# Context projections in 512-token blocks that cross batch borders, and a key-bias matmul with 128 weight rows

## The reference, cut to what matters

```python
ctx_txt = context[:, :TEXT_LEN, :]          # TEXT_LEN = 77
ctx_img = context[:, TEXT_LEN:, :]          # 179 tokens
k = (ctx_txt @ Wk).reshape(B, TEXT_LEN, HEADS, DIM_HEAD)
v = (ctx_txt @ Wv).reshape(B, TEXT_LEN, HEADS, DIM_HEAD)
k_ip = (ctx_img @ Wk_ip).reshape(B, Li, HEADS, DIM_HEAD)
v_ip = (ctx_img @ Wv_ip).reshape(B, Li, HEADS, DIM_HEAD)
...
qp = _proj(q, W1, b1, W2, b2)
kp = _proj(k, W1, b1, W2, b2)
qk = jnp.einsum('bqd,bkd->bqk', qp, kp) * scale + mask
attn = jax.nn.softmax(qk, axis=-1)
return jnp.einsum('bqk,bkd->bqd', attn, v1)
```

## Time and profile before

| | |
|---|---|
| median of 3 runs | 3375.27 us (3375.1 to 3377.76) |
| the profiled execution | 3377.16 us, of which its span 3375.4 us |
| PE busy | 3161.2 us, 94% of the span |
| PEld, DVE, ACT, POOL busy | 80%, 58%, 49%, 23% |
| projections, first matmul on a block to last | 23.3 to 445 us |
| masked attention, first turned tile to last matmul | 2328 to 2471 us |

### The profile page before, as it was taken

The page is one execution under the profiler, slowest core; times in us unless marked ns, Lnnn a source line. Parts: engine busy times, 40 slices in busy tenths (PEclk is TensorE's granted clock), DMA queues, the critical chain, the costliest instruction groups (busy, mean ns, idle before and its releaser), DMA issues. The chain is left out here.

```text
span 3375.4 us, 51188 instructions
## 1 busy us (share of the span) xinstructions
PE 3161.2 (94%) x16792; PEld 2696.3 (80%) x16792; DVE 1962.9 (58%) x3422; ACT 1667.3 (49%) x3204; POOL 789.5 (23%) x881
## 2 busy tenths in 40 slices
PE   7999979999999969999996798997979999999998
PEld 6988969999999958887884576885857888888886
DVE  3245549999999955557888995554752222222211
ACT  3132249999999943336776785564721111111110
POOL 0000038888888830000000200003700000000000
PEclk9999989999999989999997898998989999999999
DMA  6487755555555545556666686444831110001000
GB/s 187 120 253 228 224 171 165 170 177 173 170 165 173 157 150 198 179 172 203 226 218 219 215 265 218 158 161 165 251 116 60 38 35 24 31 26 38 32 25 13
DMA packets 370165, 503.46 MB, mean 149 GB/s; under 512 B 58940, under 2 KB 237420, under 8 KB 366032
## 3 DMA queue, kind: packets, MB, share of 16 engines
q1 hardware_dynamic: 356458, 473.37, 44.6%
q0 software_dynamic: 4768, 18.88, 1.7%
q10 hardware_dynamic: 8720, 8.41, 0.7%
HBM read 292.86 MB, written 174.11 MB: 138 GB/s over the span
## 5 line engine op out<-in xcount | busy, mean ns | idle before, releaser
L2592 DVE SCALAR_TENSOR_TENSOR lf_hT<-lf_hb,lf_hT 128x512 fp32r<-128x512 f32 x128 | 88.5, 691 | 571.6 <-ACT lf_hT L2668 571.6
L2668 ACT ACTIVATE lf_hT<-lf_hb 128x512 fp32r<-128x512 f32 x128 | 76.5, 598 | 669.2 <-PE lf_py L192 639.6
L768 POOL TENSOR_TENSOR at_prob<-at_prob,at_rec 128x308 f32<-128x308 f32 (+1 forms) x256 | 261.3, 1042 | 87.6 <-DVE at_rec L808 87.3
L908 ACT ACTIVATE at_prob<-at_sc,at_nm 128x77 f32<-128x77 f32 (+1 forms) x1024 | 277.6, 385 | 7.3 <-DVE at_nm L795 4.9
L190 PE MATMUL lf_hb<-lf_xT,lf_w 128*128 128x512 f32 x512 | 204.7, 400 | 1.3 <-DVE lf_hT L2592 1.3
L192 PE MATMUL lf_hb<-lf_xT,lf_w 128*128 128x512 f32 x512 | 203.5, 398 | 0.0
L190 PE MATMUL lf_py<-lf_w,lf_hT 128*128 128x512 f32 x512 | 203.1, 397 | 0.0
L192 PE MATMUL lf_py<-lf_w,lf_hT 128*128 128x512 f32 x512 | 203.1, 397 | 0.0
L191 PE MATMUL lf_hb<-lf_xT,lf_w 128*128 128x512 f32 x512 | 203.0, 396 | 0.0
L191 PE MATMUL lf_py<-lf_w,lf_hT 128*128 128x512 f32 x512 | 202.6, 396 | 0.0
L801 DVE TENSOR_REDUCE at_sums<-at_prob 128x4 f32<-128x308 f32 (+1 forms) x256 | 166.1, 676 | 17.7 <-ACT at_prob L908 17.5
(11 more groups left out here) (334 smaller groups left out, 9229.3 us busy)
## 6 DMA issues: line engine op xcount, KB each, us to landing
at_kr<-k_rows SPq DMA_DIRECT2D x256, 128.0 KB, 2.9
at_qs<-at_qst SPq DMA_DIRECT2D x512, 64.0 KB, 2.0
raw_gate<-pg_stage SPq DMA_DIRECT2D x96, 256.0 KB, 2.0
pu_rg<-raw_gate SPq DMA_DIRECT2D x96, 256.0 KB, 3.2
raw_up<-pu_stage SPq DMA_DIRECT2D x96, 256.0 KB, 2.1
om_raw<-raw_up SPq DMA_DIRECT2D x48, 512.0 KB, 4.5
dn_raw<-raw_up SPq DMA_DIRECT2D x48, 512.0 KB, 3.8
xn_parts<-pr_xturned SPq DMA_DIRECT2D x32, 512.0 KB, 5.0
```

The lines of the kernel that those rows point to most:

```text
L768: ins = pool.tensor_tensor(prob[:, i, :, lo:hi], prob[:, i, :, lo:hi], rec[:, z, g, :].unsqueeze(2).broadcast_to([P, 2 * NTE, hi - lo]), A ...
L908: ins = act.activation(prob[:, i, m, lo:hi], sc[n % 2][:, m, lo:hi], ACT.Exp, bias=nm[:, n % 2, g, m:m + 1])
L2592: dve.scalar_tensor_tensor(hT[:, i, 1, :], hb[i][:], 0.0, hT[:, i, 0, :].bitcast(F32), ALU.max, ALU.subtract).then_inc(h_done, 1)
L2668: act.activation(hT[:, m % 2, 0, :], hb[m % 2][:], ACT.Relu).then_inc(h_hi, 1)
```

## The change

Blocks no longer end with a batch: the text tokens (1232) become blocks of 512, 512 and 208, the image tokens (2864) five blocks of 512 and one of 304. Twelve blocks become nine, 168 jobs become 138, and 36 tiles become 33. The pieces of a tile now have whatever length the batch borders give. A key job is stored by one transfer for the whole batches and one more for each cut batch at its ends. The ring `stage` has 4 slots instead of 6, `xturned` 2 instead of 3. The `x` turns start with the second text block instead of the first image block, and the `w` turns stand three to a block in the last four blocks.

In the masked attention the weights `ones` have 128 rows, `trow` has 128 rows of which POOL clears all and the transfer fills two; POOL clears it ahead of its other work.

```diff
-TB, IB = 4, 2
...
 def context_blocks():
+
     blocks = []
-    for g in range(B // TB):
-        blocks.append(Rows("text", g * TB, TB * TEXT, [((g * TB + i) * S, TEXT) for i in range(TB)]))
-    for g in range(B // IB):
-        blocks.append(Rows("img", g * IB, IB * IMG, [((g * IB + i) * S + TEXT, IMG) for i in range(IB)]))
+    for kind, off, length in (("text", 0, TEXT), ("img", TEXT, IMG)):
+        every = Rows(kind, B * length, [(b * S + off, length) for b in range(B)])
+        for lo in range(0, every.n, CT):
+            n = min(CT, every.n - lo)
+            blocks.append(Rows(kind, n, [(row, count) for _, row, count in every.pieces(lo, n)]))
     return blocks
...
-    NBANK, NST, NRAW, NX = 6, 6, 3, 3
+    NBANK, NST, NRAW, NX = 6, 4, 3, 2
...
+    x_job = [first_job[1 + i] for i in range(NCH)]
+    x_by_job = {job: i for i, job in enumerate(x_job)}
+    WPER, WAT = 3, (5, 7, 11)
+    w_job = [first_job[NBLK - KF // WPER + i // WPER] + WAT[i % WPER] for i in range(KF)]
...
-    turns += [(first_job[NTX + i] + 5 + 2 * t, "x", i, t) for i in range(NCH) for t in range(NT)]
-    WFIRST, WPER, WAT = NTX + 2, KF // (NCH - 2), (6, 12)
-    turns += [(first_job[WFIRST + i // WPER] + WAT[i % WPER], "w", i, 0) for i in range(KF)]
+    turns += [(x_job[i] + 6 + 2 * t, "x", i, t) for i in range(NCH) for t in range(NT)]
+    turns += [(w_job[i], "w", i, 0) for i in range(KF)]
...
-                return [(k_d[job[1] * P:(job[1] + 1) * P, cols].rearrange("p (b n) -> p b n", n=S)[:, :, off:off + each],
-                         slot[:, 0:block.n].rearrange("p (b n) -> p b n", n=each))]
...
+                return out_ + [(k_d[rows_, row:row + count], slot[:, at:at + count]) for at, row, count in parts if count < each]
...
-        trow = ph.sb("trow", [2, B, S], F32R)
-        ones = ph.sb("ones", [2, P], F32R)
+        trow = ph.sb("trow", [P, B, S], F32R)
+        ones = ph.sb("ones", [P, P], F32R)
...
-            sp.dma_start(trow[:].bitcast(F32), split_d.rearrange("b a s -> a b s")).then_inc(t_ready, 16)
+            sp.wait_ge(trow_cleared, 1)
+            sp.dma_start(trow[0:2].bitcast(F32), split_d.rearrange("b a s -> a b s")).then_inc(t_ready, 16)
...
+            pool.memset(trow[:].rearrange("p b s -> p (b s)").bitcast(F32), 0.0).then_inc(trow_cleared, 1)
             pool.memset(ones[:].bitcast(F32), 1.0).then_inc(ones_made, 1)
```

More of the change, by code:

```diff
@@ L195, with __init__ @@
 IMG = S - TEXT
-TB, IB = 4, 2
 class Rows:
-    def __init__(self, kind, first, n, runs):
-        self.kind, self.first, self.n, self.runs = kind, first, n, runs
+    def __init__(self, kind, n, runs):
+        self.kind, self.n, self.runs = kind, n, runs
         self.tiles = [(lo, min(P, n - lo), max(0, lo + P - n)) for lo in range(0, n, P)]
@@ L246, in project_context @@
     blocks = context_blocks()
-    NBLK, NTX = len(blocks), B // TB
+    NBLK, NTX = len(blocks), sum(block.kind == "text" for block in blocks)
     jobs = [(c, job) for c, block in enumerate(blocks) for job in jobs_of_block(block)]
@@ L250, in project_context @@
     NJ = len(jobs)
-    NBANK, NST, NRAW, NX = 6, 6, 3, 3
+    NBANK, NST, NRAW, NX = 6, 4, 3, 2
     WIDE = max(b.n for b in blocks)
     MOST = max(len(b.tiles) for b in blocks)
-    assert NBLK == NTX + NCH
+    assert NBLK == NCH + 1
+    x_job = [first_job[1 + i] for i in range(NCH)]
+    x_by_job = {job: i for i, job in enumerate(x_job)}
+    WPER, WAT = 3, (5, 7, 11)
+    w_job = [first_job[NBLK - KF // WPER + i // WPER] + WAT[i % WPER] for i in range(KF)]
+    gate_load = [w_job[0] - 9, w_job[0] - 7] + [w_job[i] + 1 for i in range(KF - 2)]
     turns = [(first_job[c - 1] + 1 + t if c else -1, "c", c, t) for c in range(NBLK) for t in range(len(blocks[c].tiles))]
-    turns += [(first_job[NTX + i] + 5 + 2 * t, "x", i, t) for i in range(NCH) for t in range(NT)]
-    WFIRST, WPER, WAT = NTX + 2, KF // (NCH - 2), (6, 12)
-    turns += [(first_job[WFIRST + i // WPER] + WAT[i % WPER], "w", i, 0) for i in range(KF)]
+    turns += [(x_job[i] + 6 + 2 * t, "x", i, t) for i in range(NCH) for t in range(NT)]
+    turns += [(w_job[i], "w", i, 0) for i in range(KF)]
     turns.sort(key=lambda turn: turn[0])
@@ L318, in stores @@
                 each = TEXT if block.kind == "text" else IMG
-                off, nb = (0 if block.kind == "text" else TEXT), block.n // each
-                cols = slice(block.first * S, (block.first + nb) * S)
-                return [(k_d[job[1] * P:(job[1] + 1) * P, cols].rearrange("p (b n) -> p b n", n=S)[:, :, off:off + each],
-                         slot[:, 0:block.n].rearrange("p (b n) -> p b n", n=each))]
+                rows_ = slice(job[1] * P, (job[1] + 1) * P)
+                parts = block.pieces(0, block.n)
+                whole_ = [piece for piece in parts if piece[2] == each]
+                at, row, nb = whole_[0][0], whole_[0][1], len(whole_)
+                off = 0 if block.kind == "text" else TEXT
+                out_ = [(k_d[rows_, row - off:row - off + nb * S].rearrange("p (b n) -> p b n", n=S)[:, :, off:off + each],
+                         slot[:, at:at + nb * each].rearrange("p (b n) -> p b n", n=each))]
+                return out_ + [(k_d[rows_, row:row + count], slot[:, at:at + count]) for at, row, count in parts if count < each]
             lo, count, skip = block.tiles[job[1]]
@@ L406, in _ @@
                         load(c + 2)
-                    if j == first_job[NTX - 1]:
+                    if j == x_job[0] - 8:
                         load_x(0)
                     for i in range(KF):
-                        if j == first_job[WFIRST + i // WPER - 1] + WAT[i % WPER] + 1:
+                        if j == gate_load[i]:
                             load_gate(i)
-                    if c >= NTX and c + 1 < NBLK and j == first_job[c] + 12:
-                        load_x(c - NTX + 1)
+                    if j - 13 in x_by_job and x_by_job[j - 13] + 1 < NCH:
+                        load_x(x_by_job[j - 13] + 1)
                     for n, kind, _, _ in turns_at.get(j - 1, []):
@@ L486, in _ @@
                         job_out_of(j)
[L487 to L490, removed]
+                    if j - 4 in x_by_job:
+                        statistics(x_by_job[j - 4])
+                    if j - 5 in x_by_job:
+                        normalize(x_by_job[j - 5])
                     for i in range(KF):
-                        if j == first_job[WFIRST + i // WPER] + WAT[i % WPER] - 2:
+                        if j == w_job[i] - 2:
                             integers(i)
@@ L2025, in masked_attention @@
         r_ready, c_ready = [ph.sem(f"r_ready{i}") for i in range(NR)], [ph.sem(f"c_ready{i}") for i in range(NC)]
-        m_ready, traw_ready, t_high, t_low, t_stored, t_ready, ones_made = (
-            ph.sem(n) for n in ("m_ready", "traw_ready", "t_high", "t_low", "t_stored", "t_ready", "ones_made"))
+        m_ready, traw_ready, t_high, t_low, t_stored, t_ready, ones_made, trow_cleared = (
+            ph.sem(n) for n in ("m_ready", "traw_ready", "t_high", "t_low", "t_stored", "t_ready", "ones_made", "trow_cleared"))
         stat_done, mv_ready, var_ready, rstd_ready, shift_ready, xn_ready, spacer_d, spacer_p, spacer_a = (
```

## The result

The changed kernel takes 3428.51 us (3427.72 to 3431.56, four runs), the kernel before 3375.47: 1.0157 times as long, 95% interval 1.014 to 1.0175, or 53 us more. The forecast was 3398, slower by 22.6. The direction and the place were right and the size was less than half.

What follows compares the result with a forecast made beforehand. PE was taken to bound the kernel before, the first DMA engine the changed projections: +34 there and -11.4 from the key-bias matmul gave +22.6 us, 3398 us. The range was 3355 to 3460, the forecast's own 3382 to 3460.

Steps and rivals of the forecast that it cites:

- What bounds the kernel: Projections and masked attention: PE sets the end of both stages, as long as the ring of stores keeps up.
- part 1: Projections: fewer value jobs, turns and key-job time take 19 us off PE; a 2.6 us later start leaves 17.4.
- Part 2, the reading of the pieces: Row transfers: n rows use as many DMA engines as n's largest divisor up to 16, always the same first ones.
- Part 2, the size: Projections: work on the first DMA engine ends the stage at 479 instead of 445, 34 us longer.
- never rests: Projections: the first DMA engine, busy without pause from 25.9, is through the seventh block's 386 us of work at 412.
- 412 - 15 + 82 = 479: Projections' end: first engine through at 412, less PE's lead of 15, plus PE's 82 us for the last two blocks.
- Part 2, the place: Projections: worst are the third block (369 packets, 31 us) and the second image block (696 packets, 58 us).
- Part 3: SP in the projections: 165 issues more at 299 ns, some 50 us of SP's time, costed at nothing.
- Part 4: Masked attention: key-bias matmul on 128 rows saves 0.38 us each, 30 of 32 counting: 11.4 us off.
- Part 5: Masked attention: POOL's clearing takes 3.5 us, leaving 1.4 us before POOL is needed, so no delay.
- PE stays the bound: Rival for the projections: the first engine's work is spread otherwise or buffers carry it; -28.8 us, 3346; chance 15%.
- Worse: Rival for the projections: packets at 100 ns and more other work, stage about 570, time 3490; chance above 3460 is 7%.

Runs made afterwards that it cites:

- b2_bias: The kernel before with the key-bias change alone (ones and trow on 128 rows, trow cleared by POOL): 3368.98 us, ratio 0.9975.

## Why the prediction was right or wrong

**What bounds the kernel, and part 1: right.** PE's own steps fell by 17.5 us, where the parts said 19. The start came 1.0 later, not 2.6. That the gain is real shows where nothing stalls: with both kinds of pieces cut and the gate turns moved, the stage ends at 429.4, where the forecast had 427.6 for PE alone.

**Part 2, the reading of the pieces: right.** From two odd shares in the earlier trace rows came the rule of the largest divisor; the counts of small packets bear it out exactly, and 127 + 1 against 112 + 16 rows, 114 us apart, shows what it costs. The Trainium skill has the same rule (DMA: Bandwidth & Descriptors, section "Why a DMA increments its semaphore by 16 and not by 1"); the counts and this pair of runs agree with it on this chip. A lone engine's price is also as read. From 262 to 268 of the changed kernel only `v_rows` is issued, and 147 packets take 8.7% of 16 engines, one engine and a little. Through most of it packets of 2 KB start 80 ns apart, one behind the other. Not all of them are `v_rows`: 64 packets of 512 bytes, the size of the `xn_parts` rows, stand in the same line from 265.8 to 267.3, so it seems that the loaded engine's sixteenth of a transfer that uses all engines waits behind the few-engine pieces.

```profile
DMA packets 147, 0.19 MB, mean 31 GB/s; under 512 B 7, under 2 KB 71, under 8 KB 147
...
q1 hardware_dynamic: 147, 0.19, 8.7%
```

**Part 2, the size: wrong, +34 forecast, +59.8 measured.** The steps of the sum, one by one. The work through the seventh block was put at 386 us, done at 412 if the engine never rests. Adding up when at least one packet of the queue was under way, from the packets' records, gives 386 us of that by 425, with 13 us in which nothing moved. At that time, 424.97, the slot of the seventh block's last value job came free, with the end of a wait of DVE for `v_rows`. So the work was sized well (this count holds any engine's packets, so it is an upper bound for the first's), but "never rests" was false by 13 us. PE left its seventh block at 404.6, 20 us ahead of that point where I had 15, instead of at 397: of the 13 us, 7.6 are left as a miss. The other 18 are in the last two blocks, which I put at PE's own 82 us, and which took 100 (57.8 and 42.3): 81.0 of its own steps, 10.1 of gaps, 8.9 of small excess, of it 7.0 at the lower clock. There the backlog was still being worked off: PE's gaps of 5.9 us at 422 and 3.4 at 472 end when DVE, held in front of a slot of unstored `v_rows`, has made a piece of the gate weights, and the clock is at the lower level behind each. So in the sum's own terms 412 - 15 + 82 = 479 became 425 - 20 + 100 = 505. The term for the lower clock was left out altogether: over the whole stage the small excess at that level is 17 us more than before; at the upper level it is 4 us less, which leaves the 12.9.

So the failed step is the one that turned an engine's total work into an end time: it took the loaded engine as always busy, gave the stall's end no tail, and priced PE behind a stall at full speed.

**Part 2, the place: right.** The stores of the second image block, with its 696 packets, make the longest gap; PE stands behind DVE and ACT, and these behind `v_rows`, `k_rows` and `xn_parts`, as listed. Against the fastest kernel of the study PE's third block lost 4 us (31.1 against 27.1), the first image block 15 (62.8 against 48.0), and the third image block 29 (79.4 against 50.3).

**Part 3, SP: half wrong.** The count was wrong: the trace has 105 issues more (88 for keys, 14 for values, 3 for loads), not 165. By their number they cost nothing: with 148 still more the stage is fast. But their duration is no constant 299 ns: summed over the stage, SP's issues took 345 us instead of 161, of it 167 instead of 35 in issues over 1 us. "If SP were late, it would be late as the first engine is" held; that its lateness also keeps back other transfers was not in the sum. How much of the 63 us of gaps that makes is open: a kernel that issues the value stores from another queue wasn't run.

**Part 4: the mechanism right, 8.2 instead of 11.4.** The step is the count and what stands around the matmul: not 30 but 28 of them lie where PE doesn't wait for input, which is 0.8 of the 3.2 us (the stretch in the earlier trace rows begins with the third batch, not the second). The 28 save 10.7 at the matmul; what the stage then gives back is 8.2 in this execution and 9.2 in the mean of all traces, and the cause of that remainder stays open, the lower clock being one candidate. The Trainium skill's rule (TensorE: Matmul & The Clock Gate, section "Why this matters for your kernels": 32 rows take the time of 128) speaks of the matmul by itself. No run here shows one by itself: the own durations, 0.38 us with 2 rows and 0.28 with 128, are modelled ends. In this stream the three steps around it went from 0.74 us to 0.36, so the measured row decided, and `b2_bias` bears it out.

**Part 5: right.** The clearing takes 3.51 us, and POOL's first deviation then waits 1.95 us for DVE as it had waited 4.95:

```profile
2378.23 3.51 POOL L2120 MEMSET ma_trow<- 128x4096 f32 x1 [6.52 <-DMA x<-dn_y]
...
2383.84 0.73 POOL L2108 TENSOR_TENSOR ma_rstd<-ma_var,neghalf 128x2 f32<-128x2 f32 x1 [1.95 <-DVE ma_var L2148]
```

**The rivals.** "PE stays the bound", 3346, is near what the change gives once pieces are cut at sixteen: 3355.9, or 3353.5 with the gate turns moved. It was wrong of the kernel as written. "Worse", 3490, had part of the truth: ACT waited 52 us for the two slots of `xturned`, which it never did before, and the backlog grew, to a smaller size. But with all pieces cut ACT still waits 32 us for these slots, in a stage that is fast, so this wait by itself costs little.

## What to carry to other kernels

When a transfer's rows come from arithmetic on borders, look at the divisors of the row counts, not at the bytes: cut each piece into a multiple of sixteen rows and a rest, even at the price of one more issue, and a stage that is packed tighter keeps its gain (here 53 us lost became 20 gained). A mean DMA share says nothing of the busiest engine, and it can fall while transfers become the bound. When a stall is priced, add its tail: the buffers that must drain after it, the transfers queued behind a held issue, and the matmuls at the lower clock.

## What the runs showed of the hardware

- A transfer of n rows used as many DMA engines as the largest divisor of n up to 16: in six pairs of kernels the number of small packets changed by exactly what this rule gives (by -224 with 127 + 1 rows, +256 with 112 + 16).
- An issue instruction of SP lasted up to 7.1 us for a value store and 10.0 for a context load in the changed kernel, and 9.9 with 127 rows, against medians of 0.32 to 0.36. It did so where the pieces of few engines pile up (6.1 and 9.6 us for one row behind 127), even while the DMA share of all engines was low (8.7% over six microseconds). With 112 rows none passed 2.4.
- One 2-row matmul between 128-row ones made three steps take 0.74 us instead of 0.36; filled up with zero rows it costs a step of 0.12 like its neighbours.
- After 28 us nearly without work PE's granted clock was 0.50, the lower of its two levels, for 2.6 us, with steps of 0.43 instead of 0.23 us. Over a stage with 14 gaps the small excess at the lower level came to 18.8 us, against 1.6 before.
